# Self-attention's value products in halves, two expert products ahead of turned rows, and three more weight places in the last batch

## The chip, the cores and the metric

The kernel runs on one core of a Trainium2 chip, as one launch. The metric is the device time of that core in microseconds (us), the median of several runs. The engines of a core are TensorE (PE, with its weight loads shown as PEld), VectorE (DVE), ScalarE (ACT), GpSimd (POOL) and SyncE (SP); here SP only issues transfers.

## What is computed

One decoder layer on x of 4 batches x 512 tokens x 128 features: causal attention with one head, cross-attention with 16 heads over 154 context rows under a mask, then a self-attention block with 16 heads, rotary positions and no mask, and a mixture of 8 experts of which each token takes 2.

```python
x = x + causal(layernorm(x))
x = x + cross(layernorm(x), ctx, mask)          # 16 heads of 8 features, 154 keys
h = layernorm(x)
q, k, v = h @ Wq + bq, h @ Wk + bk, h @ Wv + bv # 16 heads of 8 features, 512 keys
q, k = rope(q), rope(k)
ao = softmax(q @ k.T / sqrt(8)) @ v
x1 = layernorm(h + ao @ Wo + bo) * g1 + be1
comb = top2(softmax(x1 @ Wg + bg))              # weights of 2 experts out of 8
y = gelu(x1 @ W1[e] + b1[e]) @ W2[e] + b2[e]    # 128 -> 512 -> 128
x = x + layernorm(x1 + sum(comb[e] * y[e])) * g2 + be2
```

## The kernel before

**Order.** Each engine's program is written out by hand; engines meet only through semaphores. A batch goes through `cross(n)` (cross-attention, then the self-attention's projections), `self_attention(n)` and `tail(n)` (output projection, gate, and the causal attention of the next batch). The experts of batch p run one batch later, in gaps that `MOE_GAPS` names: up to 15 tiles of 128 tokens (`NT` = 15, in `NG` = 4 groups of up to `YG` = 4), tiles 0 to 3 in the next batch's `cross` (gaps w3 to w5b), 4 to 7 in its self-attention (o0 to o3), 8 to 11 in its tail, 12 to 14 in the cross-attention after that. The experts of the fourth batch (index 3) have no batch to hide in and run last, one tile after the other.

**Self-attention** (L1686 to L1794). The 16 heads go in four groups g of four, and the keys in four blocks c, which makes 16 steps. Scores are made twice. The first-round scores `s1` (L1699, 32 rows of the array, for the group after) give the row maxima on VectorE (L1203), through a ring of three PSUM banks. `q2` (L1706, L1708) appends the maxima to the queries; ScalarE copies it. The second-round scores `s2` (L1720) then come out less their maximum, in banks 4 to 7, and ScalarE takes exponentials of two heads at once (L846) into `px`, which has two halves, one for each parity of c. `sums_of(m)` (L1730) multiplies the exponentials of step m by the values `vf`: four products of 512 columns, each on its own 32 columns of the array, in fp32, so eight instructions. After a group's fourth step ScalarE copies bank 3 to `ot` (L852). One step on TensorE: `keep_warm`, a filler product of 512 columns whose result nobody reads (L1348), then `s2` of two heads, `s1` twice, the whole value product of the step before, `s2` of the other two heads, `s1` twice. In a group's fourth step `q2` stands in the middle and the value product behind the second half. The filler is left out in the last group of heads, but for the last batch.

**Turned rows** (L1666). After the causal and cross-attention sums, VectorE and POOL make the layer norm of the rows, TensorE turns them (L1404), ScalarE copies them (L809), and four projections follow (L1670, L1671), which VectorE turns by the rotary angles (L1182 to L1188). Before them tile 0's `up` product is made (gap w3), between the turning and the projections tile 1's `up` and tile 0's `down` (gap w4). `up` is L1371, `down` L1385, the activation between them L674. In `cross(0)` there are no experts, and 12 and 4 fillers stand in the two gaps.

**Expert weights and rows.** SP loads a tile's weights (514 KB, L469) into one of `WSLOTS` = 5 places of `wp` when the tile five before it is through `down`, then the tile's bias row b2 (64 KB, L474) when the sum of two groups before has left its buffer. VectorE adds b2 to a group's rows (L906), SP stores them (`keep_y`, L495), and when all of a batch are stored POOL gathers them back by token (`fetch_tokens`, L598, eight gathers), VectorE mixes them (`end_step`, L1122) and the result is stored (L535).

**The last batch.** Tokens reach their tiles not through memory but through `place_tokens`: VectorE builds one-hot matrices (L1298, L1302), TensorE multiplies (L1846, L1847), ScalarE copies a group (L684). Two groups are placed before tile 0, the other two after tiles 2 and 6. SP loads tiles 0 to 4 ahead, then stores the last two groups of batch 3's rows (index 2), then goes on; behind tile 12 it waits for the result of batch 3 (L535) before it loads tiles 13 and 14. VectorE's order there: place groups 0 to 3 with the sums of batch 3 between, sum group 0, mix batch 3's rows, sum group 1, finish batch 3, sum groups 2 and 3, mix the last batch. Batches are counted from 1 in the text and from 0 in the code.

## Time and profile before

| | |
|---|---|
| median of 3 runs | 735.01 us (733.05 to 737.16) |
| profiled execution | 731.61 us, span 729.8 us |
| PE busy | 639.2 us (88%), 3790 instructions |
| DVE busy | 456.0 us (62%) |
| ACT busy | 344.2 us (47%) |
| POOL busy | 120.7 us (17%) |
| chain that ended last | PE 61%, DVE 22%, issue 6%, ACT 4%, POOL 3%, DMA 2% |
| transfers | 54.95 MB, mean 75 GB/s |

How to read it: busy time is what the instructions of an engine cover; matmuls are pipelined, so a busy PE isn't PE at its peak. "Idle before" a group is the time in which its engine stood just ahead of it, and the name behind the arrow is what ended most of it. In the timeline the brackets give the same for one instruction. PEclk is the granted TensorE clock as a share of 2.4 GHz (0.50 is 1.2 GHz). In the chain of waits a piece's length runs to the start of the next.

### The profile page before, as it was taken

The numbers are of one execution on the slowest core, as the hardware profiler recorded it, in microseconds if no ns is written. First come the engines' busy times: TensorE is split into PE (matmuls) and PEld (weight loads), VectorE is DVE, ScalarE is ACT, GpSimd is POOL, SyncE is SP. The second block draws the span as 40 slices with busy tenths as digits, with TensorE's granted clock in tenths as the row PEclk, the third lists the DMA queues.
The fourth block names the chain that finished last, engine by engine and source line by source line (L and its number), as shares of the span: only waits on it lengthen the run. The fifth ranks groups of instructions, "written<-read, shape, count | busy, mean of one in ns | idle before, by whom it ended". The sixth has DMA issues, their size and how long they took to land.

```text
span 729.8 us, 10620 instructions
## 1 busy us (share of the span) xinstructions
PE 639.2 (88%) x3790; PEld 390.5 (54%) x3798; DVE 456.0 (62%) x1119; ACT 344.2 (47%) x617; POOL 120.7 (17%) x121
## 2 busy tenths in 40 slices
PE   4899899998898999999898999999889999887940
PEld 2564454346655753368636643388447533476840
DVE  4673688737934678458826678677436777378303
ACT  0405027773044457765244567763444566542520
POOL 5100100001041100001224200030406000220414
PEclk9999999999989999999999999999999998998985
DMA  6300000001043540003252630021345500036841
GB/s 196 112 0 1 1 0 1 1 1 36 1 149 97 156 135 1 1 1 114 68 169 67 179 98 1 1 57 50 101 144 160 160 0 1 30 96 194 280 109 43
DMA packets 45084, 54.95 MB, mean 75 GB/s; under 512 B 4347, under 2 KB 35433, under 8 KB 45033
## 3 DMA queue, kind: packets, MB, share of 16 engines
q1 hardware_dynamic: 43240, 50.61, 23.8%
q0 software_dynamic: 1792, 3.67, 1.6%
q8 instruction: 30, 0.49, 0.3%
q14 instruction: 22, 0.17, 0.1%
HBM read 46.73 MB, written 7.54 MB: 74 GB/s over the span
## 4 chain that ended last, share of the span: by engine, by line
PE 61%; DVE 22%; issue 6%; ACT 4%; POOL 3%; DMA 2%; SPq 1%; POOLq 0%; ACTq 0%; DVEq 0%
PE banks L1730 9%; PE banks L1371 5%; PE banks L1720 5%; PE banks L1385 5%; PE banks L1699 4%; DVE nm L1203 3%; DVE nm L1139 3%; PE banks L1348 3%; PE banks L1681 3%; PE banks L1622 2%; PE banks L1620 2%; DVE hat L893 2%; PE banks L1639 2%; POOL rstd L566 2%; PE banks L1633 2%
## 5 line engine op out<-in xcount | busy, mean ns | idle before, releaser
L1203 DVE TENSOR_REDUCE nm<-banks 128x1 fp32r<-128x512 f32 x256 | 160.3, 683 | 41.5 <-PE banks L1699 40.4
L846 ACT ACTIVATE px<-banks 128x1024 f32<-128x1024 f32 x128 | 126.4, 1023 | 47.1 <-PE banks L1720 46.7
L674 ACT ACTIVATE hT<-banks,wp 128x128 f32<-128x128 f32 x240 | 68.3, 370 | 78.2 <-PE banks L1371 78.1
L566 POOL TENSOR_TENSOR rstd<-ve,misc 128x4 f32<-128x4 f32 x19 | 19.5, 1027 | 457.9 <-DVE ve L887 457.9
L1699 PE MATMUL banks<-kst,qst 32*128 32x512 f32 x256 | 84.3, 499 | 1.6 <-ACT kst L819 0.8
L1730 PE MATMUL banks<-px,vf 128*32 128x512 f32 x512 | 73.4, 647 | 4.8 <-ACT ot L852 3.1
L1371 PE MATMUL banks<-xT,wp 128*128 128x128 f32 x480 | 69.6, 292 | 7.9 <-DMA wp<-in_experts 4.8
L1371 PEld LDWEIGHTS banks<-xT,wp 128*128 128x128 f32 x480 | 63.0, 203 | 15.3 <-issue 9.7
L1385 PE MATMUL banks<-wp,hT 128*128 128x128 f32 x480 | 67.2, 285 | 2.2 <-ACT hT L674 2.1
L1385 PEld LDWEIGHTS banks<-wp,hT 128*128 128x128 f32 x480 | 62.0, 201 | 3.8 <-ACT hT L674 2.6
L1720 PE MATMUL banks<-q2st,kst 32*128 32x512 f32 x256 | 59.3, 513 | 0.0
L1348 PE MATMUL banks<-sel_r,eye_r 128*128 128x512 f32 x152 | 55.9, 454 | 1.6 <-ACT px L846 1.5
L1139 DVE TENSOR_REDUCE nm<-banks 128x4 fp32r<-128x616 f32 x64 | 49.3, 793 | 6.8 <-PE banks L1593 6.8
L1720 PEld LDWEIGHTS banks<-q2st,kst 32*128 32x128 f32 x256 | 22.3, 187 | 49.8 <-issue 26.2
L1162 DVE COPY ot<-banks 128x512 f32<-128x512 f32 x16 | 11.1, 692 | 55.1 <-PE banks L1622 55.1
L1699 PEld LDWEIGHTS banks<-kst,qst 32*128 32x128 f32 x256 | 33.6, 183 | 21.7 <-DVE nm L1203 10.8
L1348 PEld LDWEIGHTS banks<-sel_r,eye_r 128*128 128x128 f32 x152 | 28.4, 194 | 28.6 <-issue 19.1
L796 ACT ACTIVATE px<-banks 128x1024 f32<-128x1024 f32 x32 | 31.1, 1021 | 25.6 <-PE banks L1639 25.6
L598 POOL DMA_INDIRECT yg<-expert_rows,slot x32 | 31.3, 980 | 46.7 <-DMA expert_rows<-xs 37.9
L1593 PE MATMUL banks<-kbd,qst 128*128 128x308 f32 x128 | 35.1, 355 | 0.0
L1590 PE MATMUL banks<-mb,eye_b 128*128 128x308 bf16 x128 | 27.8, 298 | 3.0 <-DVE nm L1139 2.0
L586 POOL DMA_INDIRECT expert_tokens<-xn,slot x24 | 23.4, 977 | 40.2 <-DVE slot L1110 33.8
(273 smaller groups left out, 988.9 us busy)
## 6 DMA issues: line engine op xcount, KB each, us to landing
wp<-in_experts SPq DMA_DIRECT2D x60, 514.0 KB, 4.7
...
```

The costliest lines, as they stand in the source:

```text
L566: pool.tensor_tensor(rstd[:, n, :], ve[:, n, :], exponent, ALU.pow).then_inc(k[f"ln_rstd{n}"], 1)
L674: ins = act.activation(hT[:, n % 2, c * P:(c + 1) * P], bank[h_bank(p, i)][:, c * P:(c + 1) * P], ACT.Gelu, bias=wp[:, n % WSLOTS, 2 * FF ...
L846: act.activation(px[:, c % 2, 2 * i:2 * i + 2, :], banks[:, 4 + 2 * i:6 + 2 * i, :], ACT.Exp, scale=SCALE_H).then_inc(k["f_exp"], 1)
L1139: dve.tensor_reduce(nm[:, t, g, :].rearrange("p (b h c) -> p b h c", b=2, h=2)[:, :, :, 0], banks[:, a:a + 2, 0:2 * KC].rearrange("p b (h ...
L1203: dve.tensor_reduce(nm[:, t, g, BLK * hh:BLK * hh + 1], bank[s1_bank(g, t, i)], AX.X, ALU.max, negate=True).then_inc(k["f_max"], 1)
L1348: pe.matmul(bank[i], eye_r[:], sel_r[:, 0].rearrange("p g q -> p (g q)"), start=True, stop=True)
L1371: ins = pe.matmul(bank[h_bank(p, i)][:, c * P:(c + 1) * P], wp[:, n % WSLOTS, c * P:(c + 1) * P], xT[:, i * P:(i + 1) * P], start=True, st ...
L1385: ins = pe.matmul(dst, hT[:, n % 2, c * P:(c + 1) * P], wp[:, n % WSLOTS, FF + c * D:FF + (c + 1) * D], start=(c == 0), stop=(c == FC - 1))
L1593: ins = pe.matmul(bank[i][:, 0:2 * KC], qst[:, g, t * P:(t + 1) * P], kbd[:, g, 2 * h:2 * h + 2, :], start=False, stop=True, skip_group_ch ...
L1699: pe.matmul(bank[s1_bank(g, t, i)], qst[blk(hh), g, t * P:(t + 1) * P], kst[blk(hh), g, :], start=True, stop=True).then_inc(k["f_s1"], 1)
L1720: ins = pe.matmul(bank[4 + hh], kst[blk(hh), g, c * P:(c + 1) * P], q2st[blk(hh), g, :], start=True, stop=True)
L1730: ins = pe.matmul(bank[3][blk(hh), :], vf[:, c, HG * g + hh, :], px[:, c % 2, hh, :], start=(c == 0), stop=(c == T - 1), skip_group_check= ...
```

## The change

Value products of self-attention steps whose following group still has first-round scores are made in two halves of 256 columns, one behind each pair of `s1`; the others stay whole and stand behind the second pair. The fillers of self-attention get 256 columns instead of 512. In `cross` of batches 2 to 4, `up` of tiles 0 and 1 both stand ahead of the turned rows and `down` of tile 0 behind them; in batch 1 all sixteen fillers stand ahead. In the last batch the weights have eight places, three of them in `px`, whose tiles come first; SP loads four tiles, stores group 2 of batch 3's rows, loads four more, stores group 3, and waits for batch 3's result only behind tile 14; one group of tokens is placed before tile 0, the others behind tiles 1, 5 and 9.

```diff
@@ -132,10 +132,12 @@
 WSLOTS = 5
+WMORE = 3
 MISC = 256
...
 PLACE_BANKS = (1, 2, 4, 1)
+PLACES_BEHIND = (1, YG + 1, 2 * YG + 1)
 OUT_AFTER = 12
@@ -200,6 +202,24 @@
     return Y_BANKS[(g - GROUPS_BEFORE_F) % 2] if p == B - 1 or p == B - 2 and g >= GROUPS_BEFORE_F else Y_BANKS[0]
+def w_slot(n):
+    i = n - NT * (B - 1)
+    if i < 0:
+        return n % WSLOTS
+    return (*range(WSLOTS, WSLOTS + WMORE), *range(WSLOTS))[i % (WSLOTS + WMORE)]
+def w_loads(n):
+    return sum(w_slot(m) == w_slot(n) for m in range(n + 1))
+def w_free(n):
+    return max([m + 1 for m in range(n) if w_slot(m) == w_slot(n)], default=0)
...
@@ -399,6 +419,14 @@
         X_HEAD_BANKS = (4, 1, 2, 3)
+        def weights(n, first, last):
+            i = w_slot(n)
+            if i < WSLOTS:
+                return wp[:, i, first:last]
+            first, last = [S + WP * (i - WSLOTS) + c for c in (first, last)]
+            return px[:].rearrange("p i h s -> p (i h s)")[:, first:last]
@@ -461,13 +489,13 @@
                 n = NT * p + i
-                if n >= WSLOTS:
-                    sp.wait_ge(k["y_part"], n - WSLOTS + 1)
+                if w_free(n):
+                    sp.wait_ge(k["y_part"], w_free(n))
                 if n >= W_AHEAD and p < B - 1:
...
                 e = sp.value_load(eid[0:1, p % 2, i:i + 1], min_val=0, max_val=NE - 1)
-                sp.dma_start(wp[:, n % WSLOTS, :],
-                             experts_in[bass.DynSlice(e, 1)].rearrange("e p c -> (e p) c")).then_inc(w_in[n % WSLOTS], 16)
+                sp.dma_start(weights(n, 0, WP),
+                             experts_in[bass.DynSlice(e, 1)].rearrange("e p c -> (e p) c")).then_inc(w_in[w_slot(n)], 16)
                 g = NG * p + i // YG
@@ -522,24 +550,30 @@
                         load_expert(p, i)
-                for i in range(WSLOTS, NT):
+                ahead = WSLOTS if p < B - 1 else WSLOTS + WMORE
+                for i in range(ahead, NT):
                     load_expert(p, i)
-                    done = i - WSLOTS + 1
+                    done = i - ahead + 1
                     if done % YG == 0:
...
                         sp.dma_start(slot_no, consts["slots"]).then_inc(k["slots_loaded"], 16)
-                    if p and i == OUT_AFTER:
+                    if p and i == (OUT_AFTER if p < B - 1 else NT - 1):
                         sp.wait_ge(k["out_ready"], p)
...
                     sp.wait_ge(k["g_eid"], B)
-                    for i in range(WSLOTS):
+                    for i in range(YG):
                         load_expert(B - 1, i)
-                for g in range((NT - WSLOTS) // YG, NG):
-                    keep_y(p, g)
+                    keep_y(p, NG - 2)
+                    for i in range(YG, WSLOTS + WMORE):
+                        load_expert(B - 1, i)
+                    keep_y(p, NG - 1)
+                else:
+                    for g in range((NT - ahead) // YG, NG):
+                        keep_y(p, g)
             sp.wait_ge(k["out_ready"], B)
@@ -672,7 +706,7 @@
                         ins = act.activation(hT[:, n % 2, c * P:(c + 1) * P], bank[h_bank(p, i)][:, c * P:(c + 1) * P], ACT.Gelu,
-                                             bias=wp[:, n % WSLOTS, 2 * FF + c:2 * FF + c + 1])
+                                             bias=weights(n, 2 * FF + c, 2 * FF + c + 1))
                     ins.then_inc(k["h_act"], 1)
@@ -860,11 +894,11 @@
                 gelus(B - 2, label)
-            tokens_turned(B - 1, (0, 1))
-            for g in range(NG):
-                if 1 <= g < NG - 1:
-                    tokens_turned(B - 1, (g + 1,))
-                gelus(B - 1, range(YG * g, min(YG * (g + 1), NT)))
+            tokens_turned(B - 1, (0,))
+            for i in range(NT):
+                gelus(B - 1, (i,))
+                if i in PLACES_BEHIND:
+                    tokens_turned(B - 1, (i // YG + 1,))
@@ -1342,10 +1376,11 @@
-            def keep_warm(n, i):
+            def keep_warm(n, i, width=S):
                 for _ in range(n):
-                    pe.matmul(bank[i], eye_r[:], sel_r[:, 0].rearrange("p g q -> p (g q)"), start=True, stop=True)
+                    pe.matmul(bank[i][:, 0:width], eye_r[:], sel_r[:, 0].rearrange("p g q -> p (g q)")[:, 0:width],
+                              start=True, stop=True)
@@ -1366,9 +1401,9 @@
                     pe.wait_ge(k["h_act"], NT * p + h_free(p, i))
-                pe.wait_ge(w_in[n % WSLOTS], 16 * (n // WSLOTS + 1))
+                pe.wait_ge(w_in[w_slot(n)], 16 * w_loads(n))
                 for c in range(FC):
-                    ins = pe.matmul(bank[h_bank(p, i)][:, c * P:(c + 1) * P], wp[:, n % WSLOTS, c * P:(c + 1) * P],
+                    ins = pe.matmul(bank[h_bank(p, i)][:, c * P:(c + 1) * P], weights(n, c * P, (c + 1) * P),
                                     xT[:, i * P:(i + 1) * P], start=True, stop=True)
@@ -1383,7 +1418,7 @@
                     ins = pe.matmul(dst, hT[:, n % 2, c * P:(c + 1) * P],
-                                    wp[:, n % WSLOTS, FF + c * D:FF + (c + 1) * D], start=(c == 0), stop=(c == FC - 1))
+                                    weights(n, FF + c * D, FF + (c + 1) * D), start=(c == 0), stop=(c == FC - 1))
                 ins.then_inc(k["y_part"], 1)
@@ -1662,9 +1697,15 @@
                     turn_tokens(p, range(1, NG))
-                experts(p, "w3")
+                if p < 0:
+                    experts(p, "w3")
+                    experts(p, "w4")
+                else:
+                    up(p, 0)
+                    up(p, 1)
                 turn_rows(2, n, hat3, 0)
-                experts(p, "w4")
+                if p >= 0:
+                    down(p, 0)
                 pe.wait_ge(k["ln_T2"], n + 1)
@@ -1714,22 +1755,27 @@
                     if i == 0 and (g < G - 1 or b == B - 1):
-                        keep_warm(1, 4)
+                        keep_warm(1, 4, S // 2)
                     for q in range(2):
...
-                def sums_of(m):
+                def sums_of(m, first, last):
                     g, c = divmod(m, T)
-                    pe.wait_ge(k["f_exp"], NEXP * b + 2 * (m + 1))
-                    if c == 0 and g:
-                        pe.wait_ge(k["f_ot"], (G - 1) * b + g)
+                    if first == 0:
+                        if m == 0:
+                            pe.wait_ge(k["f_v"], b + 1)
+                        pe.wait_ge(k["f_exp"], NEXP * b + 2 * (m + 1))
+                        if c == 0 and g:
+                            pe.wait_ge(k["f_ot"], (G - 1) * b + g)
                     for hh in range(HG):
-                        ins = pe.matmul(bank[3][blk(hh), :], vf[:, c, HG * g + hh, :], px[:, c % 2, hh, :],
-                                        start=(c == 0), stop=(c == T - 1), skip_group_check=True)
-                    ins.then_inc(k["f_av"], 1)
+                        ins = pe.matmul(bank[3][blk(hh), first:last], vf[:, c, HG * g + hh, :], px[:, c % 2, hh, first:last],
+                                        start=(c == 0 and first == 0), stop=(c == T - 1), skip_group_check=True)
+                    if last == S:
+                        ins.then_inc(k["f_av"], 1)
@@ -1767,14 +1813,14 @@
                                 s1(ga, ta, 2 * i + 1)
+                            if g * T + c and ga < G:
+                                sums_of(g * T + c - 1, i * S // 2, (i + 1) * S // 2)
                             if c == T - 1 and i == 0 and g + 1 < G:
                                 q2(g + 1)
-                            if g * T + c and i == (ga >= G or c == T - 1):
-                                if g * T + c == 1:
-                                    pe.wait_ge(k["f_v"], b + 1)
-                                sums_of(g * T + c - 1)
+                            if g * T + c and ga >= G and i:
+                                sums_of(g * T + c - 1, 0, S)
                             if g * T + c == 0:
@@ -1791,7 +1837,7 @@
                                 front_scores(b + 1)
-                sums_of(G * T - 1)
+                sums_of(G * T - 1, 0, S)
@@ -1849,13 +1895,12 @@
             place_tokens(0)
-            place_tokens(1)
             for i in range(NT):
...
                     down(B - 1, i - 1)
-                if i in (YG - 2, 2 * YG - 2):
-                    place_tokens(i // YG + 2)
+                if i in PLACES_BEHIND:
+                    place_tokens(i // YG + 1)
             down(B - 1, NT - 1)
```

## Rows read from the trace of the kernel before

**Rows 1.** page, groups: count | busy us, mean ns | idle before.

```profile
L1203 DVE TENSOR_REDUCE nm<-banks 128x1 fp32r<-128x512 f32 x256 | 160.3, 683 | 41.5 <-PE banks L1699 40.4
L846 ACT ACTIVATE px<-banks 128x1024 f32<-128x1024 f32 x128 | 126.4, 1023 | 47.1 <-PE banks L1720 46.7
```

**Rows 2.** q2 to q2: us, busy PE, PEld, DVE, ACT, POOL, clock, DMA.

```profile
277.39:289.72 12.33, 11.75 (x73) 4.36 (x74) 10.02 (x17) 8.84 (x11) 0.00 (x0) 1.00 0.01 1
...
588.66:602.49 13.83, 13.25 (x73) 4.62 (x74) 10.02 (x17) 8.84 (x11) 0.00 (x0) 0.88 0.00 0
```

**Rows 3.** timeline inside the first stretch: start, length, engine.

```profile
280.34 0.18 PEld L1720 LDWEIGHTS banks<-q2st,kst 32*128 32x128 f32 x2 [0.25 <-issue]
...
280.92 1.29 DVE L1203 TENSOR_REDUCE nm<-banks 128x1 fp32r<-128x512 f32 x2 [0.86 <-PE banks L1699]
...
283.98 1.07 PE L1730 MATMUL banks<-px,vf 128*32 128x512 f32 x8 [0.39 <-ACT ot L852]
...
289.72 0.47 PE L1706 MATMUL banks<-qst,eye_r 128*128 128x512 f32 x1 [0.19 <-DVE nm L1203]
```

**Rows 4.** chain of waits in that stretch: start, us, what.

```profile
279.98 0.43 PE banks L1348
280.42 0.43 PE banks L1720 x2
...
280.85 1.00 PE banks L1730 x8
```

**Rows 5.** chain of waits, batch 4's self-attention.

```profile
590.25 1.85 PE banks L1730 x8
```

**Rows 6.** chain of waits, last batch.

```profile
672.44 0.23 PE banks L1846
...
674.28 0.89 PE banks L1371 x8
```

**Rows 7.** timeline around the turned rows of cross-attention, batch 2.

```profile
230.67 2.01 ACT L684 ACTIVATE xT<-banks,cols 128x512 f32<-128x512 f32 x3 [1.02 <-PE banks L1358]
...
234.32 1.11 PE L1404 MATMUL banks<-eye,hat 128*128 128x128 f32 x4 [1.66 <-DVE hat L893]
234.95 3.21 DVE L893 TENSOR_SCALAR hat<-xin,mean,rstd 128x128 f32<-128x128 f32 x4
...
236.96 1.89 PE L1385 MATMUL banks<-wp,hT 128*128 128x128 f32 x8
...
238.66 1.04 PE L1670 MATMUL banks<-hatT,wf 128*128 128x512 f32 x2
...
239.74 0.75 DVE L1182 SCALAR_TENSOR_TENSOR px<-banks,cols,cos 128x512 f32<-128x512 f32 x1 [1.57 <-PE banks L1670]
```

**Rows 8.** the same place in batches 3 and 4.

```profile
394.98 1.38 PE L1670 MATMUL banks<-hatT,wf 128*128 128x512 f32 x2
...
549.94 1.02 PE L1670 MATMUL banks<-hatT,wf 128*128 128x512 f32 x2
```

**Rows 9.** SP's queue in the last batch: DMA issues.

```profile
653.35 0.33 SPq L469 DMA_DIRECT2D wp<-in_experts  x1
658.47 0.33 SPq L474 DMA_DIRECT2D b2r<-in_L_ffn_b  x1
659.57 0.33 SPq L469 DMA_DIRECT2D wp<-in_experts  x1
...
665.46 1.35 SPq L495 DMA_DIRECT2D expert_rows<-xs  x2
...
696.01 0.36 SPq L469 DMA_DIRECT2D wp<-in_experts  x1
```

**Rows 10.** timeline, last batch: POOL, DVE and PE.

```profile
673.00 1.04 POOL L598 DMA_INDIRECT yg<-expert_rows,slot  x1 [22.70 <-DMA expert_rows<-xs]
...
688.40 0.67 DVE L906 TENSOR_TENSOR xs<-banks,b2r 128x512 f32<-128x512 f32 x1
...
699.64 2.05 PE L1371 MATMUL banks<-xT,wp 128*128 128x128 f32 x8 [3.78 <-DMA wp<-in_experts]
```

2 lines of the change are left out of this document (1 added, 1 removed).

## The prediction, made before the changed kernel ran

> **What bounds the kernel now.** I read the stretches first, then the chain of waits, then the timelines at the three places that the change touches. Self-attention comes first: from one `q2` to the next (four steps, a quarter of the heads) takes 12.33 us at the full clock, and no engine fills it: VectorE is busy 10.02, ScalarE 8.84 [rows 2]. VectorE's maxima (683 ns each) are the largest load, with 41.5 us idle in all, nearly all of it before a product of L1699; the exponentials (1023 ns) wait for L1720 [rows 1]. So TensorE's order feeds both unevenly. Its pieces are priced by the chain: a filler 0.43 us, a block of two second-round and two first-round score products 0.43, a value product of eight instructions 1.00 [rows 4]. While a value product runs whole, VectorE gets no new pair of scores: it idles 0.86 once per stretch and less at other steps. TensorE itself waits 0.39 for the copy of `ot` (more, since its weight load had waited already) and again before `q2`, for the last maximum [rows 3]. Pieces on TensorE: 4 x (0.43 + 2 x 0.43 + 1.00) + about 0.85 for `q2` = 10.0, against 12.33: the stretch is set by the alternation, not by one sum.
>
> The second place is the turned rows in cross-attention of batches 2 to 4: TensorE idles 1.66 for them, then runs up(1) and down(0) ahead of the projections, in batch 2 at a low rate (1.89 for eight instructions, where 0.89 is the full rate) [rows 6, 7]. The third is the last batch, where weights arrive too late: SP's queue stands 5 us behind the first bias row, and later 6 us behind the store of batch 3's result, so TensorE waits 3.78 for tile 13's weights [rows 9, 10].
>
> **Part 1: value products in halves, half fillers.** Ten of a batch's sixteen value products are split (steps 1 to 10). Half a filler: of its 0.43 us, 0.23 is the stream of 512 columns (the spacing of such products back to back [rows 6]), so half a stream saves 0.115: 0.32. Between that and 0.22 (all of it proportional) I keep 0.32, since the weight load that follows a filler stands 0.25 [rows 3], which doesn't shrink. Half a value product: eight 128-column instructions space at 0.11 each [rows 6]; of a value product four run side by side, so it streams 2 x 512 columns = 0.89, and 0.11 of its 1.00 is fixed. A half is 0.445 + 0.11 = 0.56; I use 0.57. Bounds: 0.50 (proportional) and 0.70 (a second fixed 0.14, one more standing weight load than the 0.11). TensorE's sum per split step is then 0.32 + 0.86 + 1.14 = 2.32 against 2.29: no saving by itself.
>
> The gain is in the order. I walk one stretch, zero being the start of the block behind `q2`; scores reach VectorE 0.57 after their block starts (280.35 to 280.92 [rows 3, 4]), ScalarE after 0.54; a pair of maxima takes 1.29 alone, 1.24 in a row. Second half to 1.30; filler 1.62; block 2.05; half 2.62; block 3.29 (its last product waits for the bank that VectorE frees at 2.84); half 3.86; filler and block 4.61; then the wait for `ot`, copied 4.2 to 4.8 behind the exponential: half 4.94 to 5.51; block 5.94; half 6.51; filler and block 7.26; half 7.83; block 8.49; half 9.06; filler and block 9.81; half 10.38; `q2`, whose last maximum was ready at 9.9, to 11.25. So 11.25 against 12.33: 1.09 saved. VectorE's gap of 0.86 becomes 0.33; the wait for `ot` shrinks to 0.33, the one before `q2` is filled by the half ahead of it. What is late next: TensorE's own pieces, then VectorE at about 10.4.
>
> A batch has one such stretch in full (`q2`(1) to (2)). From (2) to (3) no half stands ahead of `q2`, so it starts at 10.03: 1.43 saved. Ahead of `q2`(1) there are three split steps but the first waits for `vf` and the exponentials as before: 0.24 by the same walk. Per batch 2.76, four batches 11.0. With halves at 0.70 TensorE's pieces alone are 11.2 per stretch, and with the `ot` wait 11.9: 0.4 saved, 4 in all. With VectorE as the only bound, 10.4: 17 in all. The fillers of the last quarter, in batch 4 only, lie beside exponentials: nothing. The extra waits don't reach anyone: `f_v` is awaited at the same place, and the count that ScalarE needs of a value product is now raised half a step later, but always ahead of the block whose exponential needs it.
>
> A rule speaks against it: the Trainium skill, "TensorEngine Tiling (Array Packing)", section Key Properties, says that changing the tiling mode drains TensorE. Each split adds one such change, and the load that stands 0.25 [rows 3] agrees that it costs. The page gives no figure; by the fixed 0.11 of the row it is 40 x 0.11 = 4.4 us, which the walk already holds.
>
> **Part 2: two first products ahead of the turned rows.** up(1) needs all four turned groups; ScalarE has them at 230.67 + 2.01 = 232.68, so up(1) runs 232.8 to 233.7, inside the idle that ends at 234.32 [rows 7]. After the rows are turned (235.4) only down(0) stands before the projections, and its activations are done at 235.1: 0.89, so they start at 236.3 instead of 238.66. VectorE takes them only when its layer norm of the next batch is done (234.95 + 3.21 = 238.16), instead of 239.74: at least 1.55; up to 2.3 by the end of the rotary steps, which then run without waiting for TensorE. Batch 2: 2.0. Batch 3, projections at 394.98, has the same shape: 1.9. Batch 4 runs it at the full clock (549.94) [rows 8], and has no layer norm there: 0.8. In batch 1 four fillers move ahead of the rows, and VectorE's layer norm of batch 2 ends after both: nothing. Sum 4.7; from 2.4 (0.8 each, if the low rate comes all the same) to 6. If the idle that hides up(1) is gone, it costs its 0.89, thrice.
>
> **Part 3: the last batch.** Three weight places more, in `px`, let SP issue without waiting for products. But tile 0's bias row still waits for a bias sum of batch 3 (658.47), so tiles 1 to 7 follow from 659.57, at about 1.6 us each [rows 9]. TensorE starts up(0) behind one placed group instead of two, some 5 us earlier. That start isn't the bound: the end is. The store of batch 3's rows that frees the gathers is moved behind tiles 5 to 7: it is issued at about 670.9 instead of about 666.4, and lies behind 1.7 MB more; before, 2.8 MB from 659.57 let the gathers start at 673.00 [rows 10], so 1.7 MB are some 6 us: gathers at 678.5. They take 15.4 until VectorE reaches the second bias sum (688.40 [rows 10]), 14 if the queue is emptier. Tile 12's bias row waits for this sum, and tiles 13 and 14 stand behind it in SP's queue, now without the store of the result before them. 678.5 + 14 + 0.7 + 0.2 = 693.4, tile 13's weights 1.1 later, its product 3.6 behind (696.01 to 699.64): 698.1 instead of 699.64. I count 1.0. From 4 better (gathers not delayed) to 1.5 worse. Placing group by group adds nothing: the same 32 products. From the last product on, 23 us are the same chain as before.
>
> **Sum.** The profiled run took 731.61 (span 729.8). 11.0 + 4.7 + 1.0 = 16.7, giving 714.9 for it. The median of the runs shown is 735.01, 3.4 above; low-clock episodes like the one of [rows 5] fall differently in each run. Against the median: 718.3, so 718.
>
> **Rivals.** (a) The halves are dear (0.70): 4 + 4.7 + 1 less than 735.0, 725; with nothing from Part 1, 729. For it: eight short instructions may not space like long ones, and no row shows them. Against: groups of 128-column products hold their rate [rows 6]. (b) More than I walk: VectorE alone bounds (17 + 4.7 + 1: 712), or fewer clock episodes. One stretch with an episode takes 13.83 at a mean clock of 0.88, 1.5 us more [rows 2], and it starts behind the idle before `q2`, which goes; two or three fewer: 714. Taken together, 711. (c) Slower, by the clock: half the filler's columns go, and if TensorE is then granted 1.2 GHz for much of self-attention, a value product costs 1.85 instead of 1.00 [rows 5]. An episode costs 1.5 us for 0.12 x 13.83 / 0.5 = 3.3 us at the low level, 0.45 per us. To lose the 16.7 and 3.7 more, 20 in all, takes 44 us at the low level, 40% of the 108 us of split steps; with half of them, 24 us: 742. Against it: streamed columns per us stay level, since the stretch shortens as the fillers do. If one episode came in each of the 12 stretches, 7 more than now: 729. (d) The last batch gets worse through the late gathers, by 1.5: 721. (e) The change does nothing in self-attention since VectorE's ring of three banks splits each block: that is the end of (a).
>
> **Chances.** Forecast, its own range 714 to 724: 0.62. (a) 0.18, (b) 0.11, (c) 0.09, of which 0.06 above 735. Half a percent is 3.7 us, about what a measurement of this kernel can tell from no change. Faster takes the forecast, (b), most of (a): 0.85; same 0.09; slower 0.06. The range leaves out (c)'s upper part and the tips of (a) and (b): 711 to 730.
>
> **What would show it.** A stretch from `q2` to `q2` of 11.2 (12.3 if (a) holds, with half products spaced over 0.7); VectorE's largest gap in it near 0.6 behind `q2`; projections 1.5 to 2 us nearer to the turned rows in batches 2 and 3; the first gather of batch 3's rows at 5 us later in its place against the first up of the last batch minus 5; tile 13 still waited for. A granted clock under 0.9 in the split steps would mean (c). The forecast is wrong if the stretches keep 12.3, or if they shorten and the next stage gives it back by waiting for expert weights.

## The result, and the profile after

| | before | after |
|---|---|---|
| median of 4 runs | 734.03 us (731.56 to 737.16) | 709.54 us (706.54 to 712.63) |
| ratio to before | | 0.967, 95% interval 0.961 to 0.973 |
| profiled execution, span | 731.61, 729.8 | 712.63, 710.8 |
| mean clock of the profiled execution | 0.953 | 0.958 |
| mean clock of the other runs shown | | 0.963, 0.969, 0.969 |

Forecast were 718 us and a range of 711 to 730; the changed kernel is at 709.5, 1.5 us under the range. The sign was right, and so were the shorter steps of self-attention, but the gain was 24.5 us instead of 17. All ratios leave out executions more than 1.5% above the fastest of their kernel; the medians and the fit below hold them too, and without them no figure at equal clock moves by more than 1.5 us.

On the page of the kernel after, two groups of section 5 answer to [rows 1] (count | busy us, mean ns | idle before). Each maximum costs the same, and VectorE's idle ahead of them fell from 41.5 to 28.6 us, ScalarE's ahead of the exponentials from 47.1 to 30.2.

```profile
L1237 DVE TENSOR_REDUCE nm<-banks 128x1 fp32r<-128x512 f32 x256 | 160.4, 684 | 28.6 <-PE banks L1740 24.0
L880 ACT ACTIVATE px<-banks 128x1024 f32<-128x1024 f32 x128 | 128.7, 1025 | 30.2 <-PE banks L1761 28.4
```

From one `q2` to the next (windows: us, busy PE, PEld, DVE, ACT, POOL, clock, DMA), to be read against [rows 2]:

```profile
257.88:270.82 12.94, 11.89 (x93) 6.09 (x91) 11.39 (x19) 9.54 (x11) 0.00 (x0) 1.00 0.39 111
270.82:281.94 11.12, 11.06 (x110) 4.88 (x106) 10.04 (x17) 9.15 (x11) 0.00 (x0) 1.00 0.01 1
281.94:292.62 10.68, 10.54 (x99) 4.74 (x96) 9.74 (x17) 8.70 (x11) 0.00 (x0) 1.00 0.01 2
411.13:426.63 15.50, 14.47 (x94) 6.51 (x92) 11.51 (x19) 9.55 (x11) 0.00 (x0) 0.78 0.36 95
```

The first row runs from `q2`(0) to `q2`(1), the second from (1) to (2), 11.12 us where before took 12.33 and the walk gave 11.25, the third from (2) to (3), 10.68 (walk 10.90). The fourth is the first one's place in batch 3 with a low stretch of the clock in it: 2.56 us more for the same work. The chain of waits in batch 1 (start, us, what) shows the pieces, whose length runs to the next start:

```profile
121.71 0.31 PE banks L1382
122.02 0.43 PE banks L1761 x2
122.45 0.01 PE banks L1740 x2
122.46 0.57 PE banks L1775 x8
```

A filler takes 0.31, half a value product 0.57, both as the walk had them (0.32, 0.57). In the timeline VectorE's gap behind `q2` is 0.53 where [rows 3] has 0.86 (the walk had 0.33, the list of signs 0.6), and ScalarE waits 0.32 for the exponential there:

```profile
270.82 0.50 PE L1747 MATMUL banks<-qst,eye_r 128*128 128x512 f32 x1
...
272.21 2.69 DVE L1237 TENSOR_REDUCE nm<-banks 128x1 fp32r<-128x512 f32 x4 [0.53 <-PE banks L1740]
...
273.58 1.02 ACT L880 ACTIVATE px<-banks 128x1024 f32<-128x1024 f32 x1 [0.32 <-PE banks L1761]
```

The places of the two kernels on one scale (start in us; the last column is after minus before, and what it adds to the row above is the gain or loss of that part):

| | before | after | after - before |
|---|---|---|---|
| `q2`(3), batch 1 | 145.26 | 141.54 | -3.7 |
| projections, batch 2 | 238.66 | 231.34 | -7.3 |
| `q2`(3), batch 2 | 302.06 | 292.62 | -9.4 |
| projections, batch 3 | 394.98 | 385.52 | -9.5 |
| `q2`(3), batch 3 | 458.74 | 448.44 | -10.3 |
| projections, batch 4 | 549.94 | 538.78 | -11.2 |
| `q2`(3), batch 4 | 616.32 | 599.12 | -17.2 |
| first placing product, last batch | 657.85 | 639.01 | -18.8 |
| end of the span | 729.8 | 710.8 | -19.0 |

Nearly all of it is won in self-attention and at the turned rows; from the first placing product on, only 0.2 more comes. The turned rows of batch 3 seem to give 0.1 only: on the way to them the changed kernel has a low stretch in its tail, from 350 to 358 us, and the kernel before two shorter ones, from 303 and from 392 us. Batch 4's self-attention gives the most because before has low-clock stretches in two of its three windows (one of them is the second row of [rows 2]), after in none; batch 3's gives the least because there after has one, the fourth row above, and before none.

The last batch went nearly as forecast in its parts (chain of waits, start, us, what):

```profile
674.22 0.68 DVE xs L940
675.05 0.33 SPq L502
...
676.16 3.73 DMA wp<-in_experts
679.89 0.14 issue
680.02 2.05 PE banks L1406 x8
...
687.66 0.57 DVE xs L940
```

The gathers of batch 3's rows start at 660.39; against the first placing product that is 6.2 us later than in [rows 10] (5.5 forecast). The second bias sum comes 13.8 behind them (14 forecast), SP issues the bias row of tile 12 at 675.05, and tile 13's product starts at 680.02, 0.8 us earlier on that scale (forecast 1.5). Then the 0.8 is gone: from that product to the end of the last one it is 7.6 us at a mean clock of 0.68, before 6.9 at 0.76.

### The profile page after: what moved, and what is told of

Read it like the earlier page. It is cut to its first block, busy times and chain, and to the rows that moved or that the text cites. A ratio compares the mean times of both kernels' runs of the same rounds, so it can differ in the third digit from the quotient of the medians.

```text
span 710.8 us, 11259 instructions
## 1 busy us (share of the span) xinstructions
PE 628.3 (88%) x4110; PEld 394.7 (56%) x4118; DVE 457.2 (64%) x1119; ACT 347.3 (49%) x617; POOL 121.2 (17%) x121
## 3 DMA queue, kind: packets, MB, share of 16 engines
q1 hardware_dynamic: 43240, 50.61, 24.5%
## 4 chain that ended last, share of the span: by engine, by line
PE 61%; DVE 22%; issue 5%; POOL 4%; ACT 4%; DMA 3%; SPq 1%; POOLq 0%; DVEq 0%; ACTq 0%
PE banks L1775 10%; PE banks L1761 6%; PE banks L1406 4%; PE banks L1420 4%; PE banks L1740 4%; PE banks L1382 3%; DVE nm L1173 3%; PE banks L1722 3%; DVE hat L927 3%; PE banks L1657 2%; PE banks L1655 2%; PE banks L1674 2%; PE banks L1668 2%; POOL yg L632 2%; POOL rstd L600 2%
## 5 line engine op out<-in xcount | busy, mean ns | idle before, releaser
L1237 DVE TENSOR_REDUCE nm<-banks 128x1 fp32r<-128x512 f32 x256 | 160.4, 684 | 28.6 <-PE banks L1740 24.0
L880 ACT ACTIVATE px<-banks 128x1024 f32<-128x1024 f32 x128 | 128.7, 1025 | 30.2 <-PE banks L1761 28.4
L708 ACT ACTIVATE hT<-banks,wp 128x128 f32<-128x128 f32 x216 | 61.6, 370 | 64.8 <-PE banks L1406 64.7
L1775 PE MATMUL banks<-px,vf 128*32 128x256 f32 (+1 forms) x832 | 78.4, 449 | 2.8 <-ACT px L880 1.2
L1740 PE MATMUL banks<-kst,qst 32*128 32x512 f32 x256 | 77.6, 502 | 1.6 <-ACT kst L853 0.8
L1406 PE MATMUL banks<-xT,wp 128*128 128x128 f32 x432 | 60.7, 285 | 8.5 <-DMA wp<-in_experts 5.5
L1406 PEld LDWEIGHTS banks<-xT,wp 128*128 128x128 f32 x432 | 54.5, 196 | 15.7 <-issue 9.5
L1420 PE MATMUL banks<-wp,hT 128*128 128x128 f32 x432 | 58.7, 279 | 2.1 <-ACT hT L708 2.1
L1420 PEld LDWEIGHTS banks<-wp,hT 128*128 128x128 f32 x432 | 53.6, 194 | 3.5 <-ACT hT L708 2.7
L1382 PE MATMUL banks<-sel_r,eye_r 128*128 128x512 f32 (+1 forms) x152 | 49.3, 411 | 2.0 <-ACT px L880 1.9
L830 ACT ACTIVATE px<-banks 128x1024 f32<-128x1024 f32 x32 | 31.2, 1022 | 28.1 <-PE banks L1674 28.1
L1761 PEld LDWEIGHTS banks<-q2st,kst 32*128 32x128 f32 x256 | 22.7, 183 | 29.5 <-issue 16.7
L1775 PEld LDWEIGHTS banks<-px,vf 128*32 128x32 f32 x832 | 16.9, 108 | 30.9 <-issue 23.2
```

What stands on the lines that cost most here:

```text
L708: ins = act.activation(hT[:, n % 2, c * P:(c + 1) * P], bank[h_bank(p, i)][:, c * P:(c + 1) * P], ACT.Gelu, bias=weights(n, 2 * FF + c, 2 ...
L880: act.activation(px[:, c % 2, 2 * i:2 * i + 2, :], banks[:, 4 + 2 * i:6 + 2 * i, :], ACT.Exp, scale=SCALE_H).then_inc(k["f_exp"], 1)
L1237: dve.tensor_reduce(nm[:, t, g, BLK * hh:BLK * hh + 1], bank[s1_bank(g, t, i)], AX.X, ALU.max, negate=True).then_inc(k["f_max"], 1)
L1382: pe.matmul(bank[i][:, 0:width], eye_r[:], sel_r[:, 0].rearrange("p g q -> p (g q)")[:, 0:width], start=True, stop=True)
L1406: ins = pe.matmul(bank[h_bank(p, i)][:, c * P:(c + 1) * P], weights(n, c * P, (c + 1) * P), xT[:, i * P:(i + 1) * P], start=True, stop=True)
L1420: ins = pe.matmul(dst, hT[:, n % 2, c * P:(c + 1) * P], weights(n, FF + c * D, FF + (c + 1) * D), start=(c == 0), stop=(c == FC - 1))
```

## The measure used below: time at equal clock

Every timed execution has its mean granted TensorE clock. Of one kernel the executions lie on a line, as here (us, mean clock), the changed kernel on one chip and the kernel before on another:

```
changed kernel: 718.22 0.953   710.66 0.965   709.08 0.967   707.86 0.968   704.29 0.974
kernel before:  738.74 0.942   736.36 0.948   732.85 0.953   731.28 0.957
```

One slope fitted to all 192 executions of the runs below, with a constant of its own for each kernel on each chip, is 5.8 us for each 0.01 of mean clock (plus or minus 0.3, 1.4 us scatter). So a difference of two kernels on one chip can be cut in two: the steps, at the same mean clock (0.960 in the table), and what the clock adds. It is a cut by regression, not a measurement of the clock alone: whatever else differs from execution to execution together with the clock goes to the clock's share. The intervals are 95% and hold the fit only. "Halves only" has five executions: a sixth, of 1623.23 us, is left out of its row.

| kernel | executions | median; before, same chip | ratio, 95% | mean clock; before | equal clock | by clock |
|---|---|---|---|---|---|---|
| changed, second chip | 6 | 709.8; 732.9 | 0.965, 0.961 to 0.969 | 0.965; 0.952 | -16.5 +- 1.4 | -7.6 |
| changed, third chip | 6 | 709.0; 731.9 | 0.966, 0.962 to 0.971 | 0.966; 0.955 | -16.2 +- 1.3 | -6.0 |
| Part 1 alone | 6 | 727.2; 747.5 | 0.972, 0.965 to 0.980 | 0.954; 0.945 | -14.2 +- 1.3 | -5.6 |
| Part 1, halves only | 5 | 735.9; 747.5 | 0.989, 0.983 to 0.996 | 0.949; 0.945 | -8.5 +- 1.4 | -2.4 |
| Part 1, half fillers only | 6 | 756.7; 747.5 | 1.015, 1.008 to 1.022 | 0.927; 0.945 | -1.3 +- 1.4 | +10.1 |
| Part 2 alone | 12 | 744.4; 747.5 | 0.998, 0.993 to 1.004 | 0.946; 0.945 | -1.2 +- 1.0 | -1.1 |
| Part 3 alone | 12 | 731.2; 730.8 | 1.001, 0.998 to 1.004 | 0.955; 0.957 | -0.6 +- 1.0 | +1.2 |
| changed, whole fillers | 6 | 714.1; 730.8 | 0.975, 0.972 to 0.979 | 0.966; 0.957 | -11.7 +- 1.3 | -5.4 |
| changed, no fillers | 6 | 707.8; 730.8 | 0.965, 0.960 to 0.969 | 0.961; 0.957 | -22.1 +- 1.3 | -2.3 |
| changed, `q2` without a half | 6 | 713.6; 730.8 | 0.975, 0.970 to 0.979 | 0.967; 0.957 | -11.8 +- 1.3 | -5.8 |
| changed, Part 2 undone | 6 | 713.0; 731.9 | 0.973, 0.969 to 0.977 | 0.963; 0.955 | -14.7 +- 1.3 | -4.4 |
| changed, halves undone | 12 | 732.2; 731.9 | 0.998, 0.995 to 1.001 | 0.944; 0.955 | -5.9 +- 1.0 | +6.8 |
| changed, Part 1 undone | 12 | 729.6; 731.9 | 0.994, 0.990 to 0.997 | 0.958; 0.955 | -2.8 +- 1.0 | -1.5 |
| late bias rows | 6 | 708.2; 732.9 | 0.964, 0.960 to 0.969 | 0.960; 0.952 | -18.7 +- 1.4 | -4.9 |
| and early store | 7 | 703.4; 732.9 | 0.958, 0.953 to 0.963 | 0.961; 0.952 | -21.2 +- 1.3 | -5.1 |
| and no fillers | 6 | 700.7; 732.9 | 0.952, 0.947 to 0.957 | 0.959; 0.952 | -28.8 +- 1.4 | -4.2 |

## The experiments

**Theory A**: the change is worth its steps (16.7 us forecast), and what came on top is the clock (the granted TensorE clock), raised by Part 1. **Rivals**: B, Part 1's steps are worth more than the walk gave (no clock needed); C, Part 2 brought the clock, since the low stretches behind the turned rows of batches 2 and 3 are gone; D, the fillers can be shortened freely, since the halves only reorder.

**The parts of the change over the kernel before.** Part 1 alone (abridged: arguments and the line of the steps whose product stays whole are left out):

```diff
 for i in range(2):
     s2(g, c, i); s1(...); s1(...)
-    if g * T + c and i == (ga >= G or c == T - 1):
-        sums_of(g * T + c - 1)                                # whole
+    if g * T + c and ga < G:
+        sums_of(g * T + c - 1, i * S // 2, (i + 1) * S // 2)  # half
...
-    keep_warm(1, 4)
+    keep_warm(1, 4, S // 2)
```

> The kernel before with Part 1 alone (halves and half fillers). Theory 1 (the order): the walk holds, so 2.8 to 3.2 us per batch at the full clock, 11 to 13 in all; stretches of 11.1 and 10.7 instead of 12.33; anything beyond is the clock. Theory 2 (the clock gives as much as the order): 16 to 19 us less than before, with a granted clock of the whole run about 0.01 above that of before and no low episode in batch 4's self-attention. Rival (Part 1 gave only the walk, and the rest of the 24.5 us is Parts 2 and 3): 11 us less, clock as before.

Its two halves, first with fillers of 512 columns as before, then with whole products:

> The halves without the half fillers: fillers keep 512 columns. If the order alone makes the stretch shorter: a filler costs 0.12 us more per step, stretches of about 11.5 to 11.6, so 1.5 to 5 us slower than with half fillers (0.45 per stretch, and nothing where TensorE waits anyway). If the wider filler matters for the clock, the granted clock is higher than with half fillers and it is as fast or faster.

> Half fillers in the kernel before, value products whole. By the order: TensorE waits for the copy of ot and for the last maximum anyway, so 0 to 0.25 us per stretch, 0 to 3 us in all. By the clock rival: fewer columns at the same stretch length, so more low episodes than the five of before in self-attention: 0 to 8 us slower, granted clock below that of before.

Windows of the three kernels from `q2`(1) to (2) and from (2) to (3) of batch 2 (columns as above). Part 1 alone:

```profile
272.65:283.78 11.13, 11.07 (x110) 4.88 (x106) 10.04 (x17) 9.15 (x11) 0.00 (x0) 1.00 0.01 1
283.78:294.46 10.68, 10.54 (x100) 4.72 (x96) 9.73 (x17) 8.69 (x11) 0.00 (x0) 1.00 0.01 2
```

Halves only:

```profile
273.33:284.90 11.57, 11.57 (x110) 4.88 (x106) 10.03 (x17) 9.14 (x11) 0.00 (x0) 1.00 0.01 1
284.90:295.92 11.02, 11.02 (x99) 4.75 (x96) 9.74 (x17) 8.68 (x10) 0.00 (x0) 1.00 0.00 1
```

Half fillers only, with one of batch 3's windows at the low clock as third row:

```profile
279.52:291.72 12.20, 11.43 (x74) 4.36 (x74) 10.03 (x17) 8.85 (x11) 0.00 (x0) 1.00 0.01 1
291.72:303.95 12.23, 10.95 (x72) 4.17 (x72) 10.03 (x17) 8.84 (x11) 0.00 (x0) 1.00 0.00 0
454.85:472.25 17.40, 17.04 (x71) 5.66 (x72) 10.12 (x17) 8.74 (x11) 0.00 (x0) 0.54 0.00 1
```

Part 1 alone has the stretches of the whole change: they are its work and need nothing of the others. With 20.3 us in the medians and 0.010 of mean clock it is Theory 2 of its expectation: 14.2 at equal clock, the rest by the clock. Halves only gives 11.57 and 11.02, half fillers only 12.20 and 12.23 instead of 12.33 twice. So a shorter filler is worth 0.1 us a stretch while the value product is whole, and 0.34 to 0.45 when it is halved: with whole products the alternation sets the stretch, with halves TensorE does (busy 11.57 of 11.57). The whole kernel with halves only is 8.8 us slower in the medians than with both, 5.7 at equal clock, where at most 5 was expected. That the half fillers alone made the kernel 1.5% slower is the clock: their mean is 0.927, 17.40 us went into a stretch that takes 12.2 at the full level, and at equal clock the kernel is not slower. This is the forecast's rival (c), for the half fillers without the halves. Rival D falls.

Parts 2 and 3 alone, each the change's own lines put into the kernel before:

> Part 2 alone: up of tile 1 ahead of the turned rows. By the sum of the prediction 4.7 us less; by the trace of the changed kernel 5.35 at the projections, of which 1.3 is given back by the first q2: 4.1 less. The low clock stretches of before right behind the turned rows in batches 2 and 3 are gone. If most of it is given back in the stacks and self-attention: under 2.

> Part 3 alone: eight weight places, groups placed singly, the store of batch 3's result behind tile 14. In the trace of the changed kernel the time from the first placing product to the last product of the experts is 48.6 us as before (48.65): so no change beyond 1 us. If the prediction's 1.0 stands in runs at a higher clock: 1 less. If the earlier start counts after all: 3 to 5 less.

Neither can be told from no change. Part 2 alone gained 1.2 +- 1.0 at equal clock, Part 3 0.6 +- 1.0.

**Parts of Part 1 in the changed kernel.** Whole fillers, no fillers in self-attention, and no half product ahead of `q2`:

```diff
-    keep_warm(1, 4, S // 2)
+    keep_warm(1, 4)                                           # whole fillers
...
-    if i == 0 and (g < G - 1 or b == B - 1):                  # no fillers
-        keep_warm(1, 4, S // 2)
...
-    if g * T + c and ga < G:
+    if g * T + c and ga < G and c < T - 1:                    # q2 without a half
...
-    if g * T + c and ga >= G and i:
+    if g * T + c and (ga >= G or c == T - 1) and i:
```

> The changed kernel with fillers of 512 columns again. By the order: 0.12 us per filler that lies on TensorE's path, 10 of them per batch: up to 4.8 slower, about 3. If the wider fillers hold the clock up better than the time they cost: same or faster than the changed kernel, with a higher granted clock.

> The changed kernel without fillers in self-attention. By the order: 0.31 per step less on TensorE, stretches of 10.4 to 10.6 (VectorE 10.02 busy plus its gap behind q2): up to 3 to 5 us faster than the changed kernel, if the clock holds. Rival (the fillers carry the clock): low episodes in every self-attention, each about 1.5 us, up to 12: 5 to 15 us slower than the changed kernel.

> The changed kernel, but in a group's fourth step the value product stays whole behind the second pair, so that nothing fills the wait ahead of q2. By the order: q2 starts 0.35 earlier but a whole product stands behind it: 0 to 0.4 us per stretch slower, 0 to 3 in all, clock as in the changed kernel. By the theory that low episodes begin behind the idle ahead of q2: such episodes are back, the clock falls by 0.005 to 0.01, and it is 4 to 8 us slower than the changed kernel.

The same two windows. Without fillers:

```profile
270.31:280.92 10.61, 10.30 (x106) 4.59 (x102) 9.75 (x17) 8.99 (x11) 0.00 (x0) 1.00 0.01 2
280.92:291.22 10.30, 9.61 (x96) 4.28 (x92) 9.44 (x17) 8.67 (x11) 0.00 (x0) 1.00 0.00 0
```

`q2` without a half ahead of it:

```profile
271.01:282.56 11.55, 11.37 (x97) 4.82 (x98) 10.02 (x16) 9.04 (x11) 0.00 (x0) 1.00 0.01 1
282.56:294.09 11.53, 11.35 (x95) 4.81 (x96) 10.16 (x17) 9.03 (x11) 0.00 (x0) 1.00 0.00 0
```

A batch from `q2`(0) to (3) takes 34.74 us at the full clock in the changed kernel (12.94 + 11.12 + 10.68). With whole fillers it is 13.30 + 11.56 + 11.03, 1.15 more, four times 4.6; at equal clock the kernel lost 16.4 - 11.7 = 4.7. Without fillers 12.67 + 10.61 + 10.30, 1.16 less, 4.6 in all; 5.7 at equal clock, of which the lower clock takes most back (ratios 0.965 here, 0.965 and 0.966 for the changed kernel). With `q2` bare 12.52 + 11.55 + 11.53, 0.86 more, 3.4; measured 4.6. The stretches and the times at equal clock agree within the fit's intervals, which is what makes the measure usable. At equal clock the half ahead of `q2` is worth as much as all the narrowing of fillers (4.6 and 4.7), by the stretches a little less (3.4 and 4.6). Per stretch the run lost 0.43 and 0.85 us, more than the 0 to 0.4 that was expected. It had no low stretch in self-attention, but it doesn't test the reason that the forecast gave in (b), the idle before `q2`: in the timeline of the kernel before TensorE's product waits there for the last maximum 12 times, 4.2 us in all, in this run never, as in the changed kernel.

**Undoing parts in the changed kernel.**

```diff
-                if p < 0:                                     # Part 2 undone
-                    experts(p, "w3")
-                    experts(p, "w4")
-                else:
-                    up(p, 0)
-                    up(p, 1)
+                experts(p, "w3")
                 turn_rows(2, n, hat3, 0)
-                if p >= 0:
-                    down(p, 0)
+                experts(p, "w4")
```

> The changed kernel with the rows turned as before: behind the four rests of the third expert pair, ahead of the fourth pair. Theory A (the part is worth its waits, 2.0 + 1.9 + 0.8 us, and the changed kernel's records show 2.4 + 2.1 + 0.8 at the projections of the second to fourth batch): at equal mean clock it is 4 to 5 us slower than the changed kernel, 12 us faster than before instead of 16. Theory B (what the waits give is handed on to the next wait or to the clock, as the part alone over the kernel before showed, 744.4 against 747.5 us at a ratio of 0.998 and nothing at equal clock): under 1.5 us between the two.

> The changed kernel with value products whole (one of 512 columns a pair of heads) and the fillers of 256 columns kept. Theory A (the half fillers alone let the clock fall, and the halves bring it back, as in the run over the kernel before: mean clock 0.929 where before had 0.945, stretches of 12.20 us at the full level, ratio 1.015): the mean clock is 0.93 to 0.95, 0.01 to 0.02 under the kernel before, and the time 725 to 735 us where before has 733. Theory B (that run's clock came of where its low stretches happened to fall, and not of the pair halves and fillers): clock as before's or above it, and 718 to 724 us.

> The changed kernel without Part 1: value products whole and fillers of 512 columns, so only the turned rows and the last batch are changed. Theory A (the parts add at equal clock): 4 us faster than before at equal mean clock, mean clock as before's, ratio 0.993 to 0.996. Theory B (Parts 2 and 3 are worth nothing by themselves): ratio 0.998 to 1.002. Theory C (the clock's rise in the changed kernel comes of the turned rows' wait, behind which the kernel before has a low stretch in the second and the third batch): mean clock 0.005 to 0.01 above before's and a ratio of 0.985 to 0.99.

> The changed kernel unaltered, on the chip of these three, as the one to hold them against. Theory (time is a step sum at equal clock and 5.5 us for each 0.01 of mean clock): 16 us faster than before where both have a mean clock of 0.955, and a mean clock 0.007 to 0.012 above before's, so a ratio of 0.965 to 0.972. Rival (the clock's rise was the two chips'): clock as before's and a ratio of 0.976 to 0.98.

On the third chip the changed kernel kept its ratio (0.966) and its rise in clock. Part 1 undone leaves 2.8 +- 1.0 at equal clock (Theory A had 4); the three parts, each alone, add up to 14.2 + 1.2 + 0.6 = 16.0, the whole change is worth 16.2 and 16.5. Halves undone with half fillers kept is Theory A of its expectation: mean clock 0.944, no gain left (0.998), though at equal clock the kernel is 5.9 us ahead. Its profile shows how such a stretch begins. Windows of it, from `q2`(1) to (2), (2) to (3), and three around the fall of the clock:

```profile
120.69:132.90 12.21, 11.41 (x73) 4.34 (x74) 10.03 (x17) 8.84 (x11) 0.00 (x0) 1.00 0.00 0
132.90:150.33 17.43, 17.07 (x71) 5.66 (x72) 10.12 (x17) 8.73 (x11) 0.00 (x0) 0.54 0.01 1
...
132.90:134.00 1.10, 1.10 (x8) 0.86 (x8) 1.05 (x2) 0.67 (x2) 0.00 (x0) 1.00 0.00 0
134.00:158.00 24.00, 23.64 (x98) 7.72 (x95) 9.32 (x15) 12.97 (x15) 0.00 (x0) 0.51 0.00 1
158.00:160.00 2.00, 2.00 (x14) 0.72 (x14) 0.69 (x1) 1.38 (x2) 0.00 (x0) 0.95 0.00 0
```

In the 14 us ahead of the fall TensorE's longest wait in the timeline is the first of these two, and no other is over 0.2; the last one ahead of the fall stands at `q2`:

```profile
127.15 1.06 PE L1771 MATMUL banks<-px,vf 128*32 128x512 f32 x8 [0.38 <-ACT ot L886]
...
132.90 0.47 PE L1747 MATMUL banks<-qst,eye_r 128*128 128x512 f32 x1 [0.20 <-DVE nm L1237]
```

The clock was at 1.00 until 134 and at half of it for 24 us, with TensorE busy all through. The Trainium skill, "TensorE: Matmul & The Clock Gate", section "What's actually happening", says that the low level is the default and that activity releases it; this trace shows both levels, and a fall without a pause, after a stretch of work with small gaps (busy 11.41 of 12.21). At the full level the busy share of TensorE in the windows (1) to (2) and (2) to (3) and the mean clock of all executions, on chips with the kernel before at 0.955 or 0.957:

| kernel | busy (1) to (2) | busy (2) to (3) | mean clock |
|---|---|---|---|
| halves undone, half fillers | 11.41 of 12.21 | 10.93 of 12.22 | 0.944 |
| before | 11.75 of 12.33 | 11.30 of 12.34 | 0.955, 0.957 |
| no fillers | 10.30 of 10.61 | 9.61 of 10.30 | 0.961 |
| changed | 11.06 of 11.12 | 10.54 of 10.68 | 0.966 |
| `q2` without a half | 11.37 of 11.55 | 11.35 of 11.53 | 0.967 |
| changed, whole fillers | 11.56 of 11.56 | 11.03 of 11.03 | 0.966 |

The kernels with more gaps have the lower clock; among the last three there is no order. Six kernels prove nothing: halves only, busy 11.57 of 11.57, reached 0.949 against a kernel before of 0.945 on the first chip, less than Part 1 alone (0.954, busy 11.07 of 11.13).

Part 2, inside the changed kernel: 713.0 to 709.0 in the medians, 4.0 us, of which 1.4 +- 1.6 at equal clock. Windows from the start of cross-attention to `q2`(0), batches 2, 3 and 4. Part 2 undone:

```profile
179.62:259.48 79.86, 73.60 (x395) 48.05 (x395) 47.56 (x123) 28.91 (x59) 16.00 (x15) 0.94 0.35 105
332.40:412.21 79.81, 73.57 (x439) 49.88 (x439) 49.66 (x125) 33.54 (x72) 22.56 (x22) 0.98 0.40 117
485.54:563.76 78.22, 71.89 (x439) 48.71 (x439) 44.78 (x110) 33.59 (x72) 21.80 (x21) 1.00 0.41 120
```

The changed kernel on the same chip, batches 2 and 3:

```profile
180.42:258.53 78.11, 72.31 (x395) 46.86 (x395) 49.35 (x123) 28.91 (x59) 16.05 (x15) 0.96 0.37 107
331.44:408.80 77.36, 72.26 (x439) 48.86 (x438) 49.46 (x125) 33.54 (x72) 23.23 (x22) 1.00 0.42 121
```

and batch 4 from the profiled execution of the result:

```profile
487.00:564.37 77.37, 72.09 (x437) 48.84 (x439) 45.04 (x110) 33.49 (x72) 21.57 (x21) 1.00 0.40 121
```

1.75, 2.45 and 0.85, 5.0 us in all (forecast 2.0, 1.9, 0.8). But in batches 2 and 3 the mean clock of the windows rises too, 0.94 to 0.96 and 0.98 to 1.00: a low stretch stood behind the wait for the turned rows, and it went with the wait. In batch 4, at the full level in both, only 0.85 remains. At equal clock the difference of 1.4 is what Theory B of the expectation named, not the 4 to 5 of Theory A. Rival C is half right: this low stretch is Part 2's, but by the fit it is worth 1.6 us of clock (6.0 against 4.4), not 6. With Part 1 undone and Part 2 kept the mean clock is 0.958, before 0.955, the whole change 0.966: three quarters of the rise are Part 1's.

**Where the low stretches begin.** The profiles show it. This table counts, over the 18 profiled executions (one per kernel, three of the changed one), the low stretches that begin within 2 us behind a product, read from the clock in windows of 1 us (low: under 0.97), and gives TensorE's wait just ahead of that product in the timeline. The kernels before, with half fillers only, with Part 2 or Part 3 alone, and the two with halves or Part 1 undone have whole value products. "Without Part 2" are before, the three runs of Part 1 or its halves over it, Part 3 alone and Part 2 undone.

| product | executions | TensorE's wait ahead of it | low stretches behind it |
|---|---|---|---|
| `q2`, whole value products | 6 | 0.19 to 0.76 us, 72 of 96 times | 20 |
| `q2`, value products in halves | 12 | none, but 0.4 us, 4 times, in each of the two without fillers | 0 of 192 |
| turned rows of batches 2 to 4, without Part 2 | 6 | 1.65 to 1.70 us | 15 of 18 |
| the same, with Part 2 | 12 | 0.42 to 0.47 us | 0 of 36 |

In the changed kernel the second of these waits reads so, to be held against the 1.66 of [rows 7]:

```profile
229.43 1.10 PE L1439 MATMUL banks<-eye,hat 128*128 128x128 f32 x4 [0.44 <-DVE hat L927]
```

So each of the two parts took away a wait behind which the clock used to fall. The low stretches that are left in self-attention with halves (eight, the fourth row of the result's windows one of them) begin about 1 us behind another wait, 0.62 to 0.75 us for an exponential, in a batch's first steps. That the wait causes the fall is not shown: 52 of the 72 waits at `q2` had none behind them, and Part 2 alone, without any at the turned rows, had low stretches elsewhere and a mean clock only 0.002 above before. What decides the clock of a given execution stays open.

**The last batch.** Part 3 gave nothing by the profile: its chain still ends through tile 12's bias row, and the gathers that this row waits for in the end start 6.2 us later than before. The bias row's wait was then taken away. The bias rows of tiles 12 to 14 behind the weights of these tiles (abridged; lines in parentheses stand for code that is unchanged):

```diff
 def load_expert(p, i):
     ...
-    (wait for the group's bias sum; load the bias row of tile i)
+    if not (p == B - 1 and i >= YG * (NG - 1)):
+        load_bias(p, i, e)
+    elif i == NT - 1:
+        for j in range(YG * (NG - 1), NT): load_bias(p, j, ...)
...
                     keep_y(p, NG - 2)
+                    keep_y(p, NG - 1)                         # early store, second kernel
                     for i in range(YG, WSLOTS + WMORE):
                         load_expert(B - 1, i)
-                    keep_y(p, NG - 1)
```

> The changed kernel unaltered, on the chip that the next three run on, so that they can be held against it and not only against the kernel before. If what it gained depends on the chip's clock episodes, its ratio to the kernel before may move from 0.967 to anywhere between 0.965 (with its work at the full level: 19 to 21 us gained in the records) and 0.977 (with one more doubled episode of 3.4 us and a kernel before with one less); the stretch between two q2 products at full clock stays at 11.1 and 10.7 us wherever it runs.

> The changed kernel, but in the last batch the weights of tiles 12 to 14 are issued ahead of the bias rows of these tiles instead of behind the wait of the first of them. Theory (the chain's end is set by SP: the wait of tile 12's bias row for the second bias sum, 674.22, stands ahead of the weights of tile 13, whose product then waits until 680.02): the product of tile 13 starts right behind that of tile 12, at about 675; the last three bias rows are issued at 675 to 677.5 and land 4 us later, so the last bias sum comes at 680.6 to 682 in place of 687.66, and the end 5.5 to 7 us earlier: ratio to the kernel before about 0.958 where the changed kernel has 0.967. Rival (the end of the kernel hangs on the gathers and the transfers of the first three groups, which the weights now collide with, or on the clock, which falls again): the gathers of the third group come 1 to 3 us later and less than 2 us are left of it.

> As the one before, and the result rows of the fourth group's third are stored right behind those of the second one, ahead of the weights of tiles 4 to 7, in both batches' order on SP. Theory: the gathers of the third group (660.39 in the changed kernel) come up to 3 us earlier since the store no longer stands behind weight issues, so the mix of that group ends earlier and the second bias sum and the bias rows with it: 1 to 3 us more than the one before, ratio about 0.955. Rival: the weights of tiles 4 to 7 now stand behind the store's wait and the products wait for them: 1 to 4 us slower than the one before.

> As the one before, and without the fillers ahead of the score pairs in self-attention (the half products stay). Theory (each filler stands about 0.31 us in the step and the clock at the halves doesn't need them: the run without them had stretches of 10.61 and 10.30 us and gained 0.3 to 1 per cent over the changed kernel): 2 to 5 us more than the one before, ratio about 0.95. Rival (the fillers hold the clock up on a chip that is warmer or grants less): more low stretches in self-attention, each 1.5 us or doubled 3.5 us, and the same time as the one before or 2 us more.

On the second chip the changed kernel kept its ratio (0.965) and its stretches, 11.11 and 10.69 us. With late bias rows the last product is done at 678.67 instead of 687.62, but the last bias sum only at 682.31 instead of 687.66 (chain of waits of that kernel):

```profile
677.62 1.27 POOL yg L664
678.91 0.40 SPq L574
...
679.49 2.70 DMA expert_rows<-xs
...
682.31 0.57 DVE xs L950
682.96 2.04 DMA expert_rows<-xs
685.02 0.71 issue
685.73 1.04 POOL yg L642
```

The next wait in line took over: the sum needs the place of an earlier group's rows, whose store stands on SP behind the store of batch 3's result, which waits until GpSimd has written it (678.89). From the second bias sum to the last it is 9.84 us, in the changed kernel 13.44: 3.6 of the 5.5 to 7 expected; 2.2 +- 1.6 at equal clock, 1.6 in the medians, and the ratios' intervals overlap. The early store adds 2.5 at equal clock (703.4 against 708.2), as expected; without fillers on top it is 7.6 us better still at equal clock, and with its lower clock 700.7 us, 1.3% under the changed kernel on that chip and 4.8% under before, the fastest of all.

## Why the prediction missed

The step that failed is the clock, which the sum put at nothing for Part 1: it priced Part 1 by its shorter stretches at the full level alone (11.0), left fewer low stretches to rival (b), at 4 us, and then added 3.4 us from the profiled execution to the median. The runs showed 6.0 and 7.6 us by the clock in the fit for the whole change, Part 1 with its clock at 20 us, and a median 3.1 us under the profiled execution instead of 3.4 above. A smaller part is Part 1's steps themselves: 13.4 to 14.2 us at equal clock, so rival B of the experiments holds for some 2 to 3 us.

The walk's durations held, but for one: filler 0.31, half 0.57, stretches 11.12 and 10.68; VectorE's gap behind `q2` is 0.53, not 0.33. The forecast for the profiled execution, 714.9, was 2.3 us above its 712.63. At equal clock the change is worth 16.2 to 16.5 us, the sum said 16.7. That agreement is in part luck, since Part 1 was worth more and Part 2 less; term by term:

- **Part 1, 11.0.** Measured 14.2 +- 1.3 alone and 726.5 - 713.1 = 13.4 +- 1.4 inside the change, at equal clock. At the full level the records give 37.79 - 34.74 = 3.05 per batch, 12.2 in four; the walk gave 2.76. Both stretches were walked 0.1 and 0.2 too long. The price ended there: with its clock Part 1 is worth 727.2 against 747.5, 20 us, and 729.6 - 709.0 = 20.6 inside the change.
- **Part 2, 4.7.** 4.0 in the medians inside the change, 5.0 in the windows, but only 1.2 to 1.4 at equal clock: the forecast took the low rate at which up and down ran behind the wait [rows 7] as part of the gain and named no clock for it. Its own low end, 0.8 each where the rate is full, is what batch 4 showed.
- **Part 3, 1.0.** 0 in the profile, 0.6 +- 1.0 alone. The chain was right to 0.7 us; the last tiles then ran at a mean clock of 0.68 where before had 0.76. One step of it was luck: if 2.8 MB took the 13.4 us from 659.57 to 673.00, 1.7 MB are 8 us by proportion, not 6; the gathers came 6.2 later.
- **From the profiled execution to the median, +3.4.** The gap between one profile and the median of before was added to the changed kernel as if it were a cost of the program. For the changed kernel this distance is clock and had the other sign: its profile, 712.63 at 0.958, lies 3.1 above its median, and its other executions have 0.963 to 0.969. For before the clocks of the other executions beside this result are not on record. This alone is 6.5 us between 718.3 and 709.5, and 2.3 are the sum's own.
- **Rival (b)** had the cause, fewer clock episodes, at 0.11 and 4 us; by the fit it was worth 6.0 and 7.6 us on two chips. Its reason, the idle before `q2`, fits the table of where low stretches begin (20 behind that wait with whole products, none with halves); the runs without fillers have that wait back only 4 times each, with no fall behind it, and no other run with halves has it, so it is not proven. **Rival (c)** had the right mechanism for half fillers without halves; what it set against itself, that the stretch shortens as the fillers do, holds only with the halves (11.12 against 12.20). (a), (d) and (e) did not occur: halves space at 0.57, the stretches fell.

The rule on changing the tiling mode that stood against Part 1 cost what the walk held: half a product is 0.57 in the chain, which is 0.445 of stream and 0.125 that does not shrink (0.11 forecast).
